# A four-layer network on one core: batch 0's layernorm statistics, exp's table load and two DMA gathers are given other places

## The reference

```
x = x + memory_update(ctx_1024, layernorm(x), conv_w, conv_b)
x = x + moe0(layernorm(x))       # 8 experts, top 2, silu, hidden 128, plus a shared expert
x = x + attention(layernorm(x), ctx_1024, ctx_1024)   # 16 heads, 64 keys
x = x + moe1(layernorm(x))       # 8 experts, top 2, silu(x W1) * (x W3), hidden 384

def layernorm(x): return (x - mean(x)) / sqrt(var(x) + 1e-5)
def attention(q_in, k_in, v_in): 
    w = softmax((q_in Wq + bq)(k_in Wk + bk)^T / 8)
    return (w (v_in Wv + bv)) Wo + bo
```

## Time and profile before

| | us |
|---|---|
| three runs | 926.23, 931.65, 926.6 |
| median | 926.6 |
| the profiled execution's own time | 930.99 |
| its span, first to last instruction | 929.2 |
| PE busy | 792.1 (85%) |
| DVE busy | 509.5 (55%) |
| ACT busy | 490.0 (53%) |
| POOL busy | 429.3 (46%) |
| mean granted TensorE clock | 0.933 of 2.4 GHz |

### The profile page before, as it was taken

One profiled execution on the slowest core, in us unless ns is written; L12 is line 12 of the kernel. 1 busy time (PEld: TensorE's weight loads), 2 busy tenths in 40 slices (PEclk: granted clock), 3 DMA queues, 4 the chain that ended last, 5 costly groups with the idle time before them and its releaser, 6 DMA issues.

```text
span 929.2 us, 16520 instructions
## 1 busy us (share of the span) xinstructions
PE 792.1 (85%) x4538; PEld 684.7 (74%) x4538; DVE 509.5 (55%) x1345; ACT 490.0 (53%) x1374; POOL 429.3 (46%) x398
## 2 busy tenths in 40 slices
PE   2989883579999679999998999785789999999992
PEld 1636542479688568999987888674689999999991
DVE  5847851245265558889888878672122222244242
ACT  1458641146466468888776686341334444444440
POOL 2201657610577258988645678435552222222221
PEclk9899995589999889999998999898789999999996
DMA  8799974456699694384230244613332222256524
GB/s 260 267 298 341 318 254 144 127 163 203 156 201 242 173 333 79 62 203 84 59 115 1 80 149 137 199 47 103 97 98 75 69 67 66 70 180 200 187 89 158
DMA packets 122115, 143.02 MB, mean 154 GB/s; under 512 B 10391, under 2 KB 113612, under 8 KB 121004
## 3 DMA queue, kind: packets, MB, share of 16 engines
q1 hardware_dynamic: 90520, 92.03, 33.2%
q0 software_dynamic: 19856, 38.88, 15.4%
q10 hardware_dynamic: 11654, 11.05, 3.7%
HBM read 71.28 MB, written 70.65 MB: 153 GB/s over the span
## 4 chain that ended last, share of the span: by engine, by line
PE 54%; DVE 15%; ACT 9%; issue 7%; another core or an unknown queue 6%; DVEq 5%; DMA 2%; SPq 1%; POOL 1%; POOLq 0%; ACTq 0%
PE psum L678 29%; PE psum L1042 5%; ACT pr L1324 5%; PE psum L1047 5%; PE psum L1043 5%; DVE nmx L2013 2%; PE psum L1056 2%; DVE sm L2018 2%; PE psum L857 2%; PE psum L954 2%; DVE prl L2028 2%; PE psum L1026 2%; DVEq L2019 1%; DVE wlo L1983 1%
## 5 line engine op out<-in xcount | busy, mean ns | idle before, releaser
L628 POOL DMA_INDIRECT yk_dram<-ys,L x71 | 70.0, 986 | 202.2 <-ACT ys L1396 200.3
L566 POOL DMA_INDIRECT X<-yl_dram,slots_y x64 | 104.1, 1627 | 73.2 <-DMA yl_dram<-fy 50.8
L1042 PE MATMUL psum<-whi,xTh 128*128 x284 | 111.0, 391 | 22.8 <-ACT xTh L1378 22.7
L1324 ACT ACTIVATE pr<-psum,nmx 128x64 f32<-128x64 f32 x512 | 108.1, 362 | 35.2 <-DVE nmx L2013 35.2
L2107 DVE TENSOR_TENSOR hs<-psum,hs 128x384 f32<-128x384 f32 x71 | 39.7, 560 | 153.6 <-PE psum L1047 100.0
L678 PE MATMUL psum<-w_sb,cz 128*128 x426 | 104.7, 382 | 1.5 <-ACT ys L1396 1.2
L541 POOL DMA_INDIRECT xs_dram<-N,slots x64 | 64.3, 1005 | 87.3 <-DVEq L1681 50.6
L1043 PE MATMUL psum<-wlo,xTh 128*128 x284 | 97.8, 344 | 0.0
L608 POOL TENSOR_TENSOR pr<-pr,sm 128x1024 f32<-128x1024 f32 x32 | 63.8, 1992 | 57.5 <-DVE sm L2020 56.9
L678 PEld LDWEIGHTS psum<-w_sb,cz 128*128 128x128 f32 x426 | 75.8, 191 | 10.1 <-issue 2.6
L1047 PE MATMUL psum<-whi,xTl 128*128 x284 | 75.4, 347 | 3.4 <-DVE xTl L2126 3.4
(11 more groups left out here) (338 smaller groups left out, 1917.1 us busy)
## 6 DMA issues: line engine op xcount, KB each, us to landing
fx<-xs_dram SPq DMA_DIRECT2D x80, 130.0 KB
xs_dram<-fill SPq DMA_DIRECT2D x4, 2600.0 KB
yl_dram<-fy SPq DMA_DIRECT2D x80, 128.0 KB
xs<-xs_dram SPq DMA_DIRECT2D x71, 130.0 KB
wlo<-in_L_ffn_W_dram SPq DMA_DIRECT2D x4, 1536.0 KB, 7.2
ym<-yk_dram ACTq DMA_DIRECT2D x12, 512.0 KB
xs_dram<-cz SPq DMA_DIRECT2D x1, 5200.0 KB, 27.5
xs_dram<-cz SPq DMA_DIRECT2D x8, 650.0 KB
```

The source lines that it names most:

```text
L566: po.indirect_dma_start(X[:, t, :], None, YL[b // 2], bass.IndirectOffsetOnAxis(ap=slot_y[k][:, t:t + 1], axis=0), compute_op=ALU.add).the ...
L628: po.indirect_dma_start(YK, bass.IndirectOffsetOnAxis(ap=yid[:, j:j + 1], axis=0), ys[j % YB], None).then_inc(s[f"y_out{j % YB}"], 16)
L1042: nc.tensor.matmul(o, xTh[b][:, c, :], wh[c], start=c == 0, stop=False)
L1324: last = act(pr[b][:, S * h:S * h + S], bank[2 * b + h // 8][:, S * (h % 8):S * (h % 8) + S], ACT.Exp, bias=nmx[:, h:h + 1])
```

## The change

Three edits.

1. `routed_norm(0, 0)` and `(0, 1)` go from behind the slots into the second group's slots on DVE: one bn_stats in each of slots 18 to 25 (the first waits for `l_gb` of batch 0), and the arithmetic behind it, in place of `ln_finish`, as the three parts of `chain` behind slots 27, 31 and 35. `chain` itself is only moved up in the file; its test for `n_q` is adapted so that batch 0 doesn't signal it.
2. `table(2, ACT.Exp)` goes from the attention's begin into the loop of the slots on ACT, behind the last silu and ahead of the last two `scale`.
3. POOL issues 2 gathers from `late` in every tile, in place of 3 in tiles 0 and 1 and 2 in the others.

```
@@ POOL, attention loop
-                for _ in range(3 if n < 2 else 2):
+                for _ in range(2):
                     if late:
                         b_, k_, t_ = late.pop(0)
                         collect(b_, k_, t_, t_ + 1)
@@ ACT, routed(g)
                     if j + 1 < last_:
                         silu(j + 1)
+                    if j + 2 == LA:
+                        table(2, ACT.Exp)
                     scale(j)
@@ ACT, attention()
-                table(2, ACT.Exp)
                 for r in range(YB):
                     ac.wait_ge(s[f"ys_out{r}"], 16 * LA // YB)
@@ DVE, routed(g)
+                    i = j - LS * g - 18
+                    if g and i == 0:
+                        ve.wait_ge(s["l_gb"], 16 * BT)
+                    if g and 0 <= i < BT:
+                        row_stats(X, i, i + 1)
+                    if g and i in (9, 13, 17):
+                        chain((i - 9) // 4, ((0, BT),), 0)
@@ DVE, routed_norm(b, half)
-                if half and b == 0:
-                    ln_finish(xstats, b * BT, b * BT + BT, shifted=True)
-                    ve.sem_inc(s["n_st"], 1)
@@ DVE, behind the slots
             routed(1)
-            routed_norm(0, 0)
-            routed_norm(0, 1)
             meet()
@@ DVE, chain, moved up
+            def chain(part, spans, batch=None):
+                w = sum(w1 - w0 for w0, w1 in spans)
+                if part == 0:
+                    ln_open(spans)
+                if part == 1:
+                    ln_newton(w)
+                    ln_newton(w)
+                if part == 2:
+                    ln_newton(w)
+                    ln_close(spans, batch is not None)
+                    if batch is not None:
+                        ve.sem_inc(s["n_st"], 1)
+                    if batch not in (0, 1):
+                        ve.sem_inc(s["n_q"], 1)
```

More of the change, by code:

```diff
@@ L1983, in low @@
                 tt(wl, wl.bitcast(F32), wh.bitcast(F32), ALU.subtract).then_inc(s["w_lo"], 1)
-            def chain(part, spans, batch=None):
-                w = sum(w1 - w0 for w0, w1 in spans)
-                if part == 0:
-                    ln_open(spans)
-                if part == 1:
-                    ln_newton(w)
-                    ln_newton(w)
-                if part == 2:
-                    ln_newton(w)
-                    ln_close(spans, batch is not None)
-                    if batch is not None:
-                        ve.sem_inc(s["n_st"], 1)
-                    if batch != 1:
-                        ve.sem_inc(s["n_q"], 1)
             def attention():
```

## The result

The changed kernel takes 935.8 us (median of 15 runs, 932.4 to 940.6), the kernel before 928.8 us (15 runs, 925.7 to 935.7). The ratio is 1.0062 with a 95% interval of 1.0040 to 1.0085, so the change costs 5.8 us. The forecast was +5.0 us. It was given as 931.6 us from a median of 926.6 in three runs; with 15 runs that median is 928.8, and the 935.8 us measured lie just inside the upper end of the stated range, 926 to 936.

The account below looks back on a forecast made before the run. It took the chain as mostly PE (54%), with a serial stretch at the seam and DVE stalls over 0.83 us paid in full. -2.6 + 0.8 + 0 + 6.8 = +5.0 us on 926.6 gave 931.6 us, range 926 to 936.

Parts of the forecast that it names:

- Loop 16: Attention: DVE's first bn_stats of batch 3 waits for the last pair of gathers, now a tile later; +6.8 us.
- Rival (a): Loop 16: the gathers' collision does not happen or is hidden; -1.8 us, 924.8 us; chance 0.10.
- The seam: Between second slot group and attention: statistics moved out and table loaded earlier let xn(0) start sooner; -2.6 us.
- The slots: Second group's slots: bn_stats and the chain's three pieces mostly fit DVE's idle time; +0.8 us.
- POOL at the attention's begin: Tiles 0 and 1: one gather fewer in each frees at most 3.7 us of POOL, counted at 0.
- rival (b): Loop 17: the stall cools PE to its lower clock; over 1% slower, +10.2 us, 936.8 us; chance 0.05.
- Rival (c): Slots: pieces and eight bn_stats all on the path, 7.5 us in place of 0.8; +11.7, 938.3 us; chance 0.04.
- (d): Seam gives little or nothing, through table load or store landing; sum +6.8 us, 933.4 us; chance 0.13.

Follow-up runs that it names:

- e7: Kernel with only batch 0's bn_stats in the slots, plus four repeated bn_stats (1.4 us, no drain) behind slots 27, 31 and 35 of group two; ratio 0.9957.
- e10: Changed kernel with the chain's three pieces one slot earlier, behind slots 26, 30 and 34; ratio 1.0021 against the kernel before.
- e1: Changed kernel with 3 gathers again in tiles 0 and 1, all else kept; ratio 0.9992 against the kernel before.
- e8: Kernel with only batch 0's bn_stats in the slots, plus four repeated bn_stats and a drain behind slots 27, 31 and 35 of group two; ratio 0.9985.
- e3: Kernel before with only batch 0's eight bn_stats moved into the slots; arithmetic behind the slots, table and gathers as before; ratio 0.9945.
- e5: The rebuilt seam: kernel before with batch 0's bn_stats in the slots, arithmetic behind them, exp's table loaded behind the last scale; gathers unchanged; ratio 0.9964.
- e12: Kernel with only batch 0's bn_stats in the slots, plus four repeated bn_stats and a drain behind slots 27, 31 and 35 of group one; ratio 1.0037.
- e2: Kernel before with 2 gathers in every tile and nothing else; ratio 1.0078 against the kernel before.
- e9: Changed kernel with the first half of batch 3's statistics, reader of the last gathers, moved from loop 16 to 17; ratio 1.0013 against the kernel before.

## Why the prediction came out right, and where it didn't

The forecast was +5.0 us as -2.6 + 0.8 + 0 + 6.8. Measured, each from distances in the traces, it is -2.5 + 2.5 - 0.7 + 6.7 = +6.0, against +5.8 by the ratio. The total was close in part by luck: two terms were off by 1.7 and -0.7 us, with opposite signs, and small beside the term that decides. The same distances added up for the other kernels lie inside their intervals but for `e7` (-0.8 us, measured -1.0 to -6.9) and, by a hair, `e10` (+6.1, measured -2.0 to +6.0). In these two up to 3 or 4 us stay that this account does not explain.

**Loop 16, forecast +6.8, measured +6.7.** Every link held: the pair behind `split_low` of tile 15 (issue ends at 455.41, forecast 455.5), the landing 2.2 us later (forecast 2.2), DVE going on at 457.60 (forecast 457.7), `sums(16)` at 459.90 (forecast 460.1). Made alone, the edit gives the loss; undone, it takes the loss away; with the reader moved, the idle time goes. Rival (a) is out.

**The seam, forecast -2.6, measured -2.5.** The distance from the last `fy`'s end to `xna` fell by 2.9 us, and the load put 0.3 us ahead of the last `fy` against before (forecast 0.4 to 0.5); 2.89 less 0.34 is 2.5 us. But the step named the wrong earner. The forecast gave the gain to two edits together; the kernel with the statistics alone, and the table where it was, has the same 2.02 us. The table's edit is worth nothing at the seam, and costs its 0.3 us. The cost of the load was right: 1.28 us, and the next operation stands 0.02 us behind it, with no sign of the drain of 1.38 us that the Trainium skill ("ScalarE: Activation LUTs", What ACT_TABLE_LOAD costs) adds; here the measurement decides.

**The slots, forecast +0.8, measured +2.5.** This is the term that was mis-sized: 2.5 is the difference of the means above, 22.3 and 19.8 us, and the two profiled executions of before and after alone have 3.7 (19.34 and 23.01). The step that failed is the sentence that 1.22 us of DVE "costs nothing there", taken over to pieces that were priced as "0.3 longer". In group one, where the parts can be told apart, `shared_add` costs some 0.2 us, which appears a slot behind the rows that were counted; 1.4 us without a drain cost 0.53; and the drain at the end, which the forecast has no term for, 0.95 more, because DVE then stands for 0.8 us where it would have gone on. The idle time of 0.53 us was rightly seen as time in hand, a wait for ACT; it is too small for a piece with its tail. The eight bn_stats in slots 18 to 25, undrained and 0.42 us each, cost nothing that shows, as forecast: `fw(58)` to `fw(67)` is 13.29 us in the changed kernel and 13.84 before.

**POOL at the attention's begin, forecast 0, measured -0.7.** With one gather fewer in tiles 0 and 1, `sums(2)` to `sums(3)` falls from 8.38 to 7.71 us, and from 8.42 in `e1` to 7.71 again in after. (In the six kernels with three gathers and the arithmetic behind the slots, `sums(1)` to `sums(3)` is 17.2 to 18.1 us, against 17.75 before and 17.07 after, so the 0.7 holds for this seam.) DVE's first small operation of loop 3, before and after:

```profile
352.87 1.25 DVE L1730 TENSOR_TENSOR ta<-xstats 128x8 f32<-128x8 f32 x1
```

```profile
353.43 0.56 DVE L1735 TENSOR_TENSOR ta<-xstats 128x8 f32<-128x8 f32 x1
```

It is the same blocking by POOL's `split_low` as in the kernel with gathers in tiles 4 and 12. I read only whether the chain names POOL there, and for this it doesn't, because the time stands under DVE's name.

**PE's clock, rival (b).** The granted clock did fall. PE stood without a matmul for 4.86 us, from 454.66 to 459.52 (forecast some 5); in windows of 1 us the clock is full until 457 and at its lower level from 458 to 464. A window of after (us, then PE, PEld, DVE, ACT, POOL busy, granted clock, DMA share, GB/s):

```profile
460.50:464.50 4.00, 4.00 (x21) 4.00 (x21) 3.93 (x8) 0.77 (x4) 2.99 (x4) 0.52 0.00 0
```

For these 4 us the granted clock was 0.52 of 2.4 GHz, so nearly all of it at the lower level of 1.2. The forecast had counted on 3.6 us at that level, and it lasted between 6 and 7. Still the next step, `sums(16)` to `sums(17)`, is 7.26 us, against 7.27 before: what PE lost lay within what it had in hand, as the forecast said. Rival (c), all 7.5 us of the new work exposed, is out (2.5), and so is (d) as a cause: the gain of the seam is there.

The profiled execution of after is 8.3 us longer than that of before, not 5.8. Of the rest, 1.8 us fall between `sums(31)` and the end, where nothing was changed; the same stretch differs by more than that among kernels that are alike there (350.3 us in `e7`, 355.9 in `e8`), so I take it for the difference between executions. What stays open is why loop 22 takes 10.1 or 10.2 us in five of the kernels (`e3`, `e5`, `e7`, `e10`, `e12`; 10.3 in `e8`) and 11.2 to 11.5 in the others; DVE waits for PE's logits there, and no edit of the kernels sorts them. It may be part of what the statistics alone gained above forecast, some 1 us.

No kernel that ran has a lower ratio than the one with the statistics alone (0.9945), which is the first edit without its chain and without the other two. It and the rebuilt seam (0.9964), which the intervals don't tell apart, are the only ways that I found to keep the gain at the seam without paying for it in the slots.

## What to carry to other kernels

Before an instruction is moved on a queue, list who reads what it brings, and in which step of which loop: a slip of one tile cost 6.7 us because one wait for the whole batch stood a loop too early, and moving either side of it by one loop took that away. When work is put into an idle time, price it with what stands at its end, and follow it until the rhythm of the loop is back: a drain cost more than the length here, and part of what the length cost came three slots later. An idle time that is the same in every repetition invites a story; it is settled by the distance to the end of the work that the profile names, here 0.14 us behind ACT's silu in the kernel before, whether the idle time was 0.53 or 0.26. And when two edits aim at one wait, price each with the other already made: the table load was hidden as soon as the statistics were gone, and the chain's arithmetic nearly so.

## What the runs showed of the hardware that I had not expected

- A drain at the end of 1.4 us of DVE work cost 0.95 us a piece in the first group's slots. DVE was idle ahead of the next slot's `fw` for 0.81 to 1.08 us at 20 of 21 drained pieces (1.33 at the other), and for 0 us behind the same work without a drain, at all six.
- A DVE operation of 0.53 to 0.76 us took 1.70 to 2.42 us beside a `split_low` of POOL, and ended with it or 0.1 us later. Such time is booked as DVE's busy time; no wait shows it.
- Two issues of gathers on POOL, with no others behind them, landed 2.2 us after the end of the second issue, in each of the four kernels where DVE waited for them: after (455.41 to 457.60), `e2`, `e9` and `e10`.
